# Edge counting in a four-layer graph network kernel: the split of the first two weight matrices moves from the ends of the first and second chunk to the ends of the fourth and fifth

## What is computed

```python
h = relu(layernorm(x))                       # 625 x 512
agg = segment_sum(h[src], dst, 625)          # one sum over the edges into each node
x = x + relu((h + agg) @ W1 + b1) @ W2 + b2  # W1, W2: 512 x 512
```

## Time and profile before

| | |
|---|---|
| time, median of 3 runs | 1195.95 us (1193.87 to 1199.06) |
| the profiled execution | 1196.49 us, of which its span is 1194.7 us |
| granted TensorE clock, mean | 0.957 of full speed |
| PE busy | 1097.1 us, 92% of the span |
| DVE busy | 829.8 us, 69% |
| POOL busy | 709.1 us, 59% |
| ACT busy | 503.3 us, 42% |
| first block | until 154.97 us |

### The profile page before, as it was taken

How to read it: one execution, slowest core, us unless ns; L and a number is a source line. 1 busy time by engine, 2 the same in 40 slices (tenths; PEclk the granted TensorE clock), 3 DMA queues, 4 the chain that set the end, 5 groups by cost and what they waited for, 6 DMA issues and landing times.

```text
span 1194.7 us, 20819 instructions
## 1 busy us (share of the span) xinstructions
PE 1097.1 (92%) x6814; PEld 1006.4 (84%) x6814; DVE 829.8 (69%) x1627; ACT 503.3 (42%) x890; POOL 709.1 (59%) x958
## 2 busy tenths in 40 slices
PE   7889986859999999999999999999999999998697
PEld 6768876738998899988998889988899989998595
DVE  7999868664776556667567575765788767778524
ACT  5333343322561235521453224623577646666130
POOL 3552391434655856477555776559666875578662
PEclk9889988869999999999999999999999999999798
DMA  5000010231021221012120211222201201021101
GB/s 121 1 1 1 1 28 26 90 111 61 4 80 45 67 69 46 36 45 80 56 80 1 81 46 45 71 99 77 96 2 36 71 2 44 1 71 37 36 1 43
DMA packets 39353, 56.93 MB, mean 48 GB/s; under 512 B 13829, under 2 KB 14079, under 8 KB 38877
## 3 DMA queue, kind: packets, MB, share of 16 engines
q1 hardware_dynamic: 39252, 55.63, 14.5%
HBM read 51.48 MB, written 4.13 MB: 47 GB/s over the span
## 4 chain that ended last, share of the span: by engine, by line
PE 65%; POOL 5%; DVE 4%; issue 2%; ACT 1%; POOLq 0%; DVEq 0%; ACTq 0%
PE ps L313 40%; PE ps L1603 8%; PE ps L335 7%; PE ps L1916 3%; PE ps L1897 3%; PE ps L2079 2%; PE ps L1577 1%; PE ps L1863 1%; POOL w_lo L353 1%; POOL prob L432 1%; POOL rinv L426 1%; DVE stats L357 1%; POOL w_hi L350 1%; ACT prob L409 1%; POOL res L1284 0%
## 5 line engine op out<-in xcount | busy, mean ns | idle before, releaser
L353 POOL TENSOR_TENSOR w_lo<-w_raw,w_hi 128x512 fp32r<-128x512 f32 x152 | 201.2, 1324 | 12.7
L313 PE MATMUL ps<-yt_hi,w_hi 128*128 128x314 f32 x640 | 201.6, 315 | 3.9 <-DVE yt_lo L1981 3.8
L313 PE MATMUL ps<-yt_hi,w_lo 128*128 128x314 f32 x640 | 197.6, 309 | 0.0
L313 PE MATMUL ps<-yt_lo,w_hi 128*128 128x314 f32 x640 | 197.4, 308 | 0.0
L432 POOL TENSOR_SCALAR prob<-prob,rinv 125x628 f32<-125x628 f32 x160 | 126.8, 794 | 104.3 <-DVE rinv L417 86.0
L376 ACT ACTIVATE pt_hi<-ps 125x625 fp32r<-125x625 f32 x160 | 109.2, 694 | 102.9 <-PE ps L335 101.7
L661 PE MATMUL ps<-oh_s,oh_d 125*125 125x314 bf16 x800 | 127.6, 321 | 23.3 <-DVE oh_s L559 21.0
L661 PEld LDWEIGHTS ps<-oh_s,oh_d 125*125 125x125 bf16 x800 | 113.6, 148 | 37.1 <-DVE oh_s L559 30.2
L350 POOL TENSOR_SCALAR w_hi<-w_raw 128x512 fp32r<-128x512 f32 x152 | 96.4, 635 | 70.1 <-DMA w_raw<-L_gnn_wo 36.9
L313 PEld LDWEIGHTS ps<-yt_hi,w_hi 128*128 128x128 f32 x640 | 121.7, 190 | 6.6 <-issue 3.6
L313 PEld LDWEIGHTS ps<-yt_hi,w_lo 128*128 128x128 f32 x640 | 121.7, 190 | 0.0
(11 more groups left out here) (290 smaller groups left out, 2842.7 us busy)
## 6 DMA issues: line engine op xcount, KB each, us to landing
w_raw<-L_gnn_m_w SPq DMA_DIRECT2D x8, 1024.0 KB, 5.3
w_raw<-L_gnn_W SPq DMA_DIRECT2D x6, 1024.0 KB, 5.5
w_raw<-L_gnn_wv SPq DMA_DIRECT2D x4, 1024.0 KB, 6.1
w_raw<-L_gnn_wq SPq DMA_DIRECT2D x4, 1024.0 KB, 5.5
w_raw<-L_gnn_wk SPq DMA_DIRECT2D x4, 1024.0 KB, 7.4
w_raw<-L_gnn_wo SPq DMA_DIRECT2D x4, 1024.0 KB, 5.9
w_raw<-L_gnn_Wv SPq DMA_DIRECT2D x2, 1024.0 KB, 5.7
w_raw<-L_gnn_Wq SPq DMA_DIRECT2D x2, 1024.0 KB, 5.3
```

The lines of the kernel that those rows point to most:

```text
L313: ins = pe.matmul(out_ap, lhs(i, kk), rhs(j, kk), start=kk == 0 and n == 0, stop=kk == count - 1 and n == 2)
L353: pool.tensor_tensor(w[slot][1][:, kk, 0:cols], w_raw[slot][:, kk, 0:cols], w[slot][0][:, kk, 0:cols].bitcast(FP32), ALU.subtract).then_in ...
```

## The change

GpSimd runs the split of W1 after `add(3)` and that of W2 after `add(4)`. The instructions, their operands, the loads and the semaphores stay as they are; only their place in POOL's order is another. No other engine's stream changes.

```diff
             for c in range(CHUNKS):
                 add(c)
-                if c < 2:
-                    pool.wait_ge(s_wl[c], 16)
-                    split_weights(pool, steps, c, s_ws0[c])
+                if c >= CHUNKS - 2:
+                    n = c - (CHUNKS - 2)
+                    pool.wait_ge(s_wl[n], 16)
+                    split_weights(pool, steps, n, s_ws0[n])
```

## The result

The time after is 1199.31 us (median of 17 runs, 1194.84 to 1204.05), beside 1194.42 us for the kernel before on the same chip (17 runs, 1193.47 to 1199.06). The ratio is 1.0034, with an interval from 1.0021 to 1.0047: about 4.1 us longer, 2.5 to 5.6. That is slower, but by less than the 0.5% taken as no change, and inside the range forecast. A second comparison gives 1.0030 (1.0013 to 1.0046), which includes the forecast of +2.28 us; the first just doesn't.

A forecast was written before the change was run, and what follows sets the result against it. The prediction took DVE, slowed beside GpSimd's splits, and a block's end that holds every engine as the bounds. Terms -3.84 - 5.74 + 4.64 + 7.22 = +2.28 us gave 1198.2 us, range 1193.5 to 1202.5.

The forecast's parts named there:

- second chunk: First block: without W1's split this stretch should take the fourth chunk's 26.80 us, a saving of 3.84 us.
- third chunk: First block: without W2's split this stretch should fall from 33.17 to 27.43 us, a saving of 5.74 us.
- fourth chunk: First block: nothing is taken from or added to this stretch, so its term is 0.
- fifth chunk: First block: W1's split, added after `add(3)`, delays DVE's last one-hot and the work behind it by 4.64 us.
- after the last add: First block's end: W2's split runs on POOL alone, so the second block begins 7.22 us later for every engine.
- The reading of what bounds: First block: a split's price is DVE's time, and the block's end holds every engine until the last is done.
- the clock's 0.93: Second and third chunk: how soon PE's clock comes back after a split, taken as worth 0.93 us either way.
- The tail: First block's end, up to the second block's start: W2's split after the last add lengthens it by 7.22 us.
- A: Block's end does not hold the others for POOL, so the last term is hidden: sum -4.94, 1191.0 us; chance 0.05.
- B: Counting is not freed: savings are 0 and the two new terms stay, +11.86, 1207.8 us; chance 0.07.
- C: Second block: after PE's longer gap the clock returns one window later, up to +3, 1201.2 us; chance 0.08.
- D: Fifth chunk absorbs its split through the eight-tile ring, so the 4.64 goes: sum -2.4, 1193.6 us; chance 0.07.

The follow-up runs named there:

- after_again: The changed kernel run once more with no edit, for a second profile; 1199.35 us, ratio 1.0030 to the kernel before.
- after_third: The changed kernel run again with no edit, for a third profile; 1198.94 us.
- none: Kernel before with neither split on GpSimd; ScalarE copies the raw weights into both parts instead, so the product is not the reference's; 1187.27 us, ratio 0.9923.
- second_block: Both splits moved into the second block, with PE waiting for each before its use, against the kernel before; 1195.04 us, ratio 0.9991.
- before_delay: Kernel before with only four GpSimd memsets of a scratch tile added at the first block's end; 1199.93 us, ratio 1.0038.
- before_again: The kernel before run once more with no edit, for a second profile; 1196.02 us, ratio 0.9999.
- after_warm: Changed kernel plus 80 matmuls of unread results on PE after the last count; 1198.04 us, ratio 1.0017 to the kernel before.
- w1_fourth_only: Changed kernel without W2's split; ScalarE copies raw W2 into both parts, so the product is not the reference's; 1192.77 us, ratio 0.9964 to the kernel before.
- w1_moved_w2_kept: Kernel before with only W1's split moved to the fourth chunk's end, W2's left at the second's; 1197.38 us, ratio 1.0008.

## Why the prediction held, point by point

The forecast was +2.28 us, by a sum of five terms. By the means of the table, before against after:

```
                      forecast   bounds           measured
second chunk          -3.84      -4.8 to -2.9     26.06 - 31.16 = -5.10
third chunk           -5.74      -6.4 to -4.8     27.10 - 31.88 = -4.78
fourth chunk           0                          26.78 - 27.05 = -0.27
fifth chunk           +4.64      +3.84 to +5.5    27.47 - 22.70 = +4.77
after the last add    +7.22      +7.2 to +8.2     11.47 -  3.97 = +7.50
sum                   +2.28                                       +2.12
```

The second block's start moves by +2.36 us, from 154.40 to the 156.75 of after, after_again and after_third. That this is so near the forecast is in part chance: the three first chunks of after took 0.48 us more, nearly all of it after_third's, and the three fifth chunks of plain before average 23.22, not 22.70.

*The reading of what bounds* held. The savings are real when the splits are away (none: 9.2 us by the ratio; second_block: the first block 9.4 us shorter). DVE's instructions have the stretched lengths wherever a split runs, and it is DVE's time that a split costs. And the block's end holds every engine (before_delay).

*Second and third chunk* are mis-sized, and the two errors nearly cancel, by luck. The second saved 1.26 more than forecast, beyond its bound: 0.52 of that is that the one profile's 30.64 lay under the mean of 31.16, and 0.74 that I took the fourth chunk's 26.80 for what it does without a split, where it takes 26.06. The third saved 0.96 less: 1.29 because the profile's 33.17 was the longest of five by 1.5 us, less 0.33 because it comes out at 27.10 and not 27.43. Both terms were differences of single executions, and the bounds, drawn from the clock's 0.93 alone, held none of this spread. The working for the third chunk, that 0.63 us of DVE's lateness pass through, was not right in its parts either: the first one-hot starts 0.98 us before the mark and not 1.74 (57.70 against 58.68), the first unpack 3.56 after it and not 2.80. DVE was later than said, and the stretch was still a little shorter; on average it is 27.10 beside the fourth's 26.78, so that 0.3 us pass through.

*Fifth chunk.* Right to 0.13 us. DVE's end was rightly worked out: last one-hot 26.67 us after the mark, forecast 26.69, and all six profiles with W1's split there say 27.46 or 27.47 for the stretch. What it was compared with was a lucky pick: without a split the five executions of before's order take 21.93 to 24.17 us, and the profile's 22.85 lies 0.15 from their mean. The rows of DVE say why they vary. These are the waits in before_again's fifth chunk, but for one of 1.03 us near its start that every profile has, and then the last one-hot of before_delay, whose fifth chunk has no wait but that one:

```profile
140.94 0.38 DVE L556 TENSOR_SCALAR oh_d<-node,dstf 125x628 bf16<-125x628 f16 x1 [0.60 <-PE ps L661]
...
141.99 0.38 DVE L556 TENSOR_SCALAR oh_d<-node,dstf 125x628 bf16<-125x628 f16 x1 [0.39 <-PE ps L661]
...
142.66 0.38 DVE L556 TENSOR_SCALAR oh_d<-node,dstf 125x628 bf16<-125x628 f16 x1 [0.29 <-PE ps L661]
...
144.66 0.38 DVE L556 TENSOR_SCALAR oh_d<-node,dstf 125x628 bf16<-125x628 f16 x1 [0.29 <-PE ps L661]
```

```profile
144.41 0.36 DVE L562 TENSOR_SCALAR oh_s<-node,srcm,srcv 125x314 bf16<-125x314 f16 x1
```

In after DVE never waits for PE in this chunk beyond that first time. Compared with before_delay, where it doesn't either, its last one-hot comes 26.67 - (144.41 - 123.27) = 5.53 us later, and the stretch is 27.47 - 21.94 = 5.53 us longer. That is the 5.5 of the prediction's bound for a loss of which nothing is made good. The rule of the Trainium skill ("SBUF — State Buffer", "Who interferes with whom"), that the two engines exclude each other for a whole instruction, again agrees with the lengths, 0.74 us beside 0.62 and 1.35 beside 1.26, and also with this 5.5. The term of 4.77 is smaller because some executions of before lose time to PE in this chunk, and a split uses that time up; not because DVE wins some of its own loss back, as the choice of 4.64 below the bound of 5.5 supposes.

*The tail.* +7.50 for +7.22: the split itself takes 155.20 - 147.22 = 7.98 us here and not 7.76, its first `w_hi` 0.85 and not 0.62, and the restart 0.31 and not 0.25.

*The rivals.* A is refuted: no engine starts before POOL's end, the wait of SP is 124.8 us, and the four memsets of before_delay, which nobody needs, hold all engines as well. B is refuted by the 25.4 to 27.2 us of all stretches without a split in after's order, and by none. C is refuted for its price in the second block: PE idled for 11.55 us, but in after the granted clock is 0.50 in the block's first 2 us, 0.61 in the next 2 and 1.00 from there, no later than in before (0.50 for 4 us, 0.54 in the next 2); with a warm clock the transposes are shorter and nothing behind them is sooner. D is refuted by 27.47 against 21.93 to 24.17.

*What stays open.* The medians differ by 4.9 and 3.6 us in the two comparisons, the marks by 2.1 to 2.4. Over the two comparisons, 29 executions of after have a mean of 1199.3 us and the 42 of before beside them 1195.8, which is 3.6 us; spreads of 2.56 and 1.83 us make that uncertain by about 1.1 (two standard errors). The forecast's +2.28 lies just under the lower end. The profiled executions of after lay low among its runs: the first had the lowest span of all, 1193.1. So about 1 us more than the marks account for is probably real, and where it lies can't be said: the second block of all four profiles in after's order has its short length, nothing in the change touches what is behind the first block, and behind the second the three profiles of after take 935.6 us on average, those of before 935.1. That the longer idling of PE costs something outside these profiles isn't excluded: after_warm, with the gap filled, has a mean 1.4 us lower, and w1_fourth_only is further from after in time than its profile shows. No run settles it.

w1_fourth_only leaves the split of W2 out, so no kernel of these runs that does all the work beats the kernel before. w1_moved_w2_kept and second_block are at its level.

## What to carry to other kernels

Where all engines meet at a block's end, work that one engine does after the others are done costs nearly its whole length (here 7.5 of the 7.98 us of a split), however little anybody needs it; before moving work to the end of an engine's list, look at who finishes last there. Work on GpSimd beside a DVE that is already busy throughout costs DVE's time (5.5 us for a split of 7.8, where DVE bounds), so moving it from one such place to another (the fifth chunk, or the masks in the second block) moves the price and doesn't remove it. And a term that is the difference of two stretches of one profile should carry the spread of such stretches, which here was 1.2 to 2.2 us for the same code.

## What the runs showed of the hardware

In the second block the granted clock took different courses on the same instructions. In the 8 us that begin 71 us into the block it was 0.98 to 1.00 in eight profiles, 0.68 and 0.70 in two and 0.60 to 0.63 in three, the mean clock over the 71 us before being 0.87 to 0.90 in all of them. The block is 102.6 to 102.9 us long in the first, 104.4 and 104.6 in the second and 106.6 to 106.8 in the third. What decides between them these runs don't show.

A split on GpSimd beside a DVE that never waits costs DVE 5.5 us, of the split's 7.8: six profiles have 27.46 or 27.47 us for the fifth chunk with one, and the three in which DVE doesn't wait for PE without one have 21.93 to 21.95.

A clock that was kept up across the gap between blocks (1.00 in the second block's first 2 us and not 0.50) made 20 transposes 2.42 us long and not 4.11, with no gain behind them, because PE then waited 1.95 us for DVE.
